# A Griffin block with two MLPs: the first chunk taken by pairs of token tiles, the second chunk's mixing put behind the first gate product

## The reference

```
t   = rmsnorm(x) * n1
xb  = causal_conv4(t @ Wx) + conv_b
r,i = sigmoid(xb @ Wa), sigmoid(xb @ Wi)
a   = exp(-8 * softplus(lam) * r)
h_t = a_t * h_(t-1) + sqrt(max(1 - a_t^2, 1e-12)) * i_t * xb_t
mix = (h * gelu(t @ Wy)) @ Wo ;  h1 = x + mix
u   = rmsnorm(h1) * n2
f   = (gelu(u @ Wg) * (u @ Wu)) @ Wd
x1  = layernorm(x + h1 + f)
out = layernorm(x1 + relu(x1 @ W1 + b1) @ W2 + b2)
```

## Time and profile before

| | us |
|---|---|
| median of 3 runs | 626.53 (626.53 to 627.58) |
| the profiled execution | 628.97 |
| its span | 627.2 |
| TensorE busy | 604.5 (96%) |
| VectorE busy | 386.0 (62%) |
| ScalarE busy | 305.7 (49%) |
| GpSimd busy | 204.4 (33%) |

### The profile page before, as it was taken

One profiled execution on the slowest core, in us unless ns is written; L12 is line 12 of the kernel. 1 busy time (PEld: TensorE's weight loads), 2 busy tenths in 40 slices (PEclk: granted clock), 3 DMA queues, 4 the chain that ended last, 5 costly groups with the idle time before them and its releaser, 6 DMA issues.

```text
span 627.2 us, 9436 instructions
## 1 busy us (share of the span) xinstructions
PE 604.5 (96%) x3633; PEld 537.1 (86%) x3633; DVE 386.0 (62%) x689; ACT 305.7 (49%) x564; POOL 204.4 (33%) x305
## 2 busy tenths in 40 slices
PE   7999988999999999999999999999999999999984
PEld 6898877788988898889888898889988898988974
DVE  5795665736485747747477566848368474562554
ACT  4774733366443754447443754438444653322341
POOL 4614117220724045140723125231531314240131
PEclk9999989999999999999999999999999999999998
DMA  8600001000000001010010101001000100010001
GB/s 276 219 2 33 1 2 34 0 1 2 33 1 1 33 1 36 2 34 0 1 34 2 34 1 34 0 1 35 2 1 0 34 2 1 0 35 1 1 33 35
DMA packets 13069, 15.69 MB, mean 25 GB/s; under 512 B 584, under 2 KB 12256, under 8 KB 13024
## 3 DMA queue, kind: packets, MB, share of 16 engines
q1 hardware_dynamic: 13024, 15.09, 7.1%
HBM read 10.89 MB, written 4.19 MB: 24 GB/s over the span
## 4 chain that ended last, share of the span: by engine, by line
PE 85%; DVE 8%; ACT 2%; POOL 2%; issue 2%; DMA 1%; POOLq 0%; ACTq 0%; DVEq 0%
PE psum L284 18%; PE psum L286 17%; PE psum L285 17%; PE psum L292 10%; PE psum L294 10%; PE psum L293 10%; PE psum L299 3%; DVE xb L733 1%; DVE row L808 1%; POOL normed L1047 1%; DVE xv L769 1%; DMA xs<-in_L_attn_x_dram 1%; DVE gu_raw L831 1%; POOL rstd L1016 1%; DVE sp L971 0%
## 5 line engine op out<-in xcount | busy, mean ns | idle before, releaser
L1076 POOL TENSOR_SCALAR gu_hi<-gu_raw 128x512 fp32r<-128x512 f32 x64 | 50.6, 791 | 320.0 <-DVE gu_raw L831 320.0
L841 DVE TENSOR_TENSOR hid_lo<-hid_raw,hid_hi 128x512 fp32r<-128x512 f32 x64 | 51.6, 807 | 97.1 <-ACT hid_hi L612 97.1
L608 ACT ACTIVATE hid_raw<-psum,vecs 128x512 f32<-128x512 f32 x64 | 43.9, 686 | 128.4 <-PE psum L286 128.3
L831 DVE TENSOR_TENSOR gu_raw<-psum,gu_raw 128x512 f32<-128x512 f32 x64 | 44.1, 689 | 81.5 <-PE psum L286 79.1
L292 PE MATMUL psum<-w_d_hi,gu_hi 128*128 128x256 f32 x256 | 73.2, 286 | 2.4 <-DVE gu_lo L836 2.4
L292 PE MATMUL psum<-w_hi,hid_hi 128*128 128x256 f32 x256 | 72.1, 282 | 2.4 <-DVE hid_lo L841 2.4
L294 PE MATMUL psum<-w_d_hi,gu_lo 128*128 128x256 f32 x256 | 72.4, 283 | 0.0
L293 PE MATMUL psum<-w_d_lo,gu_hi 128*128 128x256 f32 x256 | 72.1, 282 | 0.0
L294 PE MATMUL psum<-w_hi,hid_lo 128*128 128x256 f32 x256 | 71.9, 281 | 0.0
L293 PE MATMUL psum<-w_lo,hid_hi 128*128 128x256 f32 x256 | 71.8, 280 | 0.0
L599 ACT ACTIVATE gu_raw<-psum 128x512 f32<-128x512 f32 x64 | 38.0, 595 | 49.7 <-PE psum L286 49.0
(11 more groups left out here) (145 smaller groups left out, 1544.8 us busy)
## 6 DMA issues: line engine op xcount, KB each, us to landing
xs<-in_L_attn_x_dram SPq DMA_DIRECT2D x8, 512.0 KB, 3.5
out_dram<-row SPq DMA_DIRECT2D x16, 256.0 KB, 2.2
raw<-in_L_ffn_W_dram SPq DMA_DIRECT2D x2, 1024.0 KB, 13.0
raw_gud<-in_L_attn_Wg_dram SPq DMA_DIRECT2D x1, 1024.0 KB, 9.0
raw_gud<-in_L_attn_Wu_dram SPq DMA_DIRECT2D x1, 1024.0 KB, 11.0
raw_gud<-in_L_attn_Wd_dram SPq DMA_DIRECT2D x1, 1024.0 KB, 13.6
raw_xyai<-in_L_attn_Wx_dram SPq DMA_DIRECT2D x1, 256.0 KB, 2.7
raw_xyai<-in_L_attn_Wy_dram SPq DMA_DIRECT2D x1, 256.0 KB, 2.9
```

Of the source, the lines that this page charges most:

```text
L608: nc.scalar.activation(hid_raw[:, w % SLOTS, :], bank[:, :], ACT.Relu, bias=vec("b1", m)).then_inc(relu_ready, 1)
L831: nc.vector.tensor_tensor(gu_raw[:, r % SLOTS, :], up_bank(r)[:, :], gu_raw[:, r % SLOTS, :], ALU.mult).then_inc(gu_ready, 1)
L841: nc.vector.tensor_tensor(hid_lo[:, w % SLOTS, :], hid_raw[:, w % SLOTS, :], hid_hi[:, w % SLOTS, :].bitcast(FP32), ALU.subtract).then_inc ...
L1076: nc.gpsimd.tensor_scalar(gu_hi[:, r % SLOTS, :], gu_raw[:, r % SLOTS, :], 1.0, 0.0, ALU.mult, ALU.add).then_inc(gu_hi_ready, 1)
```

## The change

- x of the first chunk is loaded as two halves, each of two token tiles. Squares, mean and power, normalising (now on VectorE), transposes and splits go by such pairs, so that a bank holds both blocks of features of a pair (`transposed_by_pairs`, `split_hi_by_pairs`, `split_lo_by_pairs`, `pair_bank`). The same is done for u of the first chunk, normalised on ScalarE (`first_norm_u`).
- The order of the first chunk's products becomes x, decay, input, y. `first_decay` takes both outputs' first block ahead of the second; `first_out` does so for each pair of tiles. The convolution finishes feature block 0 before block 1's last taps.
- ScalarE does tanh, exp, tanh, square root and GELU of the first chunk in that order, and the square of the decay moves to VectorE (`squared_decay`).
- The splits of Wy, Wa, Wi, Wg and Wu move from GpSimd to ScalarE for their high part; the softplus steps and low parts are spread between VectorE's other steps.
- `mix_x(1)` goes between the gate and the up product of unit 0, `mix_y(1)` behind the up product, `mix_decay(1)` and `mix_input(1)` behind the products of round 2, `mix_out(1)` in round 6. `down(7)` goes ahead of `gate_up(8)`.
- Fillers, in steps of `keep_running`: 8, 14, 5, 9, 28, 24 before; 10, 8, 6, 9, 36, 28, 16, 6, 10 after.

The core of the diff:

```diff
+            def transposed_by_pairs(src, ready, done, bank, fillers):
+                for q in range(PAIRS):
+                    pe.wait_ge(ready, 2 * q + 2)
+                    for tt in (2 * q, 2 * q + 1):
+                        for f in range(KD):
+                            last = nc.tensor.transpose(pair_bank(bank, q)[:, f, (tt % 2) * P:(tt % 2 + 1) * P],
+                                                       src[:, tt, f * P:(f + 1) * P], ident[:, :])
+                    last.then_inc(done, 1)
+                    keep_running(fillers[q], DOWN)
...
+            def first_decay(bank):
+
+                for k in range(KD):
+                    pe.wait_ge(xb_lo_ready, k + 1)
+                    for m in range(KD):
+                        last = product_step(psum[bank + m][:, :], "a", m, k, mT_hi, mT_lo)
+                        if k == KD - 1:
+                            last.then_inc(wa_done, 1)
...
+                if r == 0:
+                    split_done("g")
                 product(gate_bank(r)[:, :], "g", m, uT_hi, uT_lo).then_inc(gate_done, 1)
+                if r == 0:
+
+                    mix_x(1)
+                    split_done("u")
...
+                if r == KH:
+
+                    down(r - 1)
                 if units(r):
                     gate_up(r)
+                if r == 0:
+                    pe.wait_ge(gy_ready, KD)
+                    mix_y(1, bank=DOWN)
+                if r == 2:
+                    mix_decay(1)
+                    mix_input(1)
+                if r == 6:
+                    mix_out(1)
...
-            transpose_t(0)
-            keep_running(5, SECOND)
+            transposed_by_pairs(normed, t_ready, tT_done, MIX, (6, 9))
             split_done("x")
             mix_x(0)
+            keep_running(36, SECOND)
+            split_done("a")
+            pe.wait_ge(vecs_ready, 1)
+            first_decay(GATE)
+            split_done("i")
+            mix_input(0, bank=SECOND)
+            transpose_t(1)
             split_done("y")
             mix_y(0, bank=DOWN)
-            transpose_t(1)
-            keep_running(9, SECOND)
-            split_done("a", "i")
-            pe.wait_ge(vecs_ready, 1)
-            mix_decay(0, bank=GATE)
-            mix_input(0, bank=SECOND)
-            mix_x(1)
-            pe.wait_ge(gy_ready, KD)
-            mix_y(1, bank=DOWN)
             pe.wait_ge(tanh_a_ready, KD)
             keep_running(28, GATE)
             split_done("o")
-            mix_out(0, bank=GATE)
             pe.wait_ge(tanh_i_ready, KD)
-            keep_running(24, SECOND)
-            transpose_u(0)
-            mix_decay(1, bank=SECOND)
-            pe.wait_ge(gy_ready, 2 * KD)
-            mix_input(1, bank=DOWN)
-            split_done("g", "u")
+            first_out(SECOND)
+            pe.wait_ge(gy_ready, KD)
+            keep_running(16, DOWN)
+            transposed_by_pairs(normed, u_ready, uT_done, GATE, (6, 10))
```

In the rounds, ScalarE and VectorE have:

```diff
                     if m == 0:
+                        conv_start(n, 0)
+                        conv_start(n, 1)
+                        gelu_y(n, bank=DOWN)
+                    if m == 1:
+                        weight_hi("2")
+                        xb_hi(n)
+                    if m == 2:
+                        tanh_decay(n)
                         exp_decay(n)
+                        tanh_input(n)
                         square_decay(n)
                         act.preload_act_table(ACT.Gelu_apprx_tanh)
...
                 if r == 0:
+                    convolve(n, 0)
+                if r == 1:
+                    convolve(n, 1)
+                if r == 3:
                     gated_input(n)
                 if r == 4:
+                    for k in range(KD):
+                        scan(n, k)
+                gate_lo(r)
+                if r == 1:
+                    convolve(n, 2)
+                    xb_lo(n)
+                if r == 2:
+                    weight_lo("2")
+                if r == 4:
                     gated(n)
+                if r == 5:
                     hy_lo(n)
                 if r == 7:
                     weight_lo("1", ks=[0])
```

More of the change, by code:

```diff
@@ L157, in griffin_mlp_kernel @@
         x_loaded = [sem(f"x_loaded{i}") for i in range(2)]
+        x0_loaded = [sem(f"x0_loaded{q}") for q in range(PAIRS)]
         out_stored = [sem(f"out_stored{i}") for i in range(2)]
@@ L325, in mix_x, with first_out @@
                     product(psum[MIX + m][:, :], "x", m, tT_hi, tT_lo).then_inc(wx_done, 1)
+            def first_decay(bank):
[5 more added lines that the diff above has]
+                            last.then_inc(wa_done, 1)
+            def first_out(bank):
+                for q in range(PAIRS):
+                    for k in range(KD):
+                        if q == 0:
+                            pe.wait_ge(hy_lo_ready, k + 1)
+                        for tt in (2 * q, 2 * q + 1):
+                            last = product_by_tokens(half_bank(bank, tt), "o", k, mT_hi[:, k, toks(tt)],
+                                                     mT_lo[:, k, toks(tt)], k == 0 and tt % 2 == 0, k == KD - 1)
+                    last.then_inc(wo_done, 1)
             def mix_decay(c, bank=MIX):
@@ L523, in split_hi, with split_hi_by_pairs @@
                     nc.scalar.activation(dst[:, f, :], psum[MIX + f][:, :], ACT.Copy).then_inc(ready, 1)
+            def split_hi_by_pairs(dst, bank, done, ready):
+                for q in range(PAIRS):
+                    act.wait_ge(done, q + 1)
+                    nc.scalar.activation(dst[:, :, half(q)], pair_bank(bank, q), ACT.Copy).then_inc(ready, 1)
             def conv_start(c, m):
@@ L723, in split_lo, with split_lo_by_pairs, first_norm_t, squared_decay @@
                                             ALU.subtract).then_inc(ready, 1)
+            def split_lo_by_pairs(dst, hi, bank, hi_ready, ready):
+                for q in range(PAIRS):
+                    dve.wait_ge(hi_ready, q + 1)
+                    nc.vector.tensor_tensor(dst[:, :, half(q)], pair_bank(bank, q), hi[:, :, half(q)].bitcast(FP32),
+                                            ALU.subtract).then_inc(ready, 1)
+            def first_norm_t():
+                for q in range(PAIRS):
+                    dve.wait_ge(rms1_rstd, q + 1)
+                    for tt in (2 * q, 2 * q + 1):
+                        nc.vector.tensor_scalar(normed[:, tt, :], xs[0][:, tt, :], rstd1[:, tt:tt + 1], None,
+                                                ALU.mult).then_inc(t_ready, 1)
+            def squared_decay():
+                dve.wait_ge(xtail_saved, 1)
+                for m in range(KD):
+                    dve.wait_ge(a_ready, m + 1)
+                    nc.vector.tensor_tensor(xv[:, m, 0:T], decay[:, m, :], decay[:, m, :],
+                                            ALU.mult).then_inc(a_squared, 1)
+                    room(0, [m])
             def convolve_half(c, step, m):
@@ L745, in xb_lo, with room @@
                                             ALU.subtract).then_inc(xb_lo_ready, 1)
-            def room(c):
-                for m in range(KD):
+            def room(c, ms=range(KD)):
+                for m in ms:
                     dve.wait_ge(a_squared, 2 * c + m + 1)
@@ L969, in _ @@
             lam_stepped(nc.vector.tensor_scalar(poly, z, 1.0 / 17.0, None, ALU.mult))
-            for odd in range(15, 1, -2):
+            for odd in range(15, 5, -2):
+                lam_stepped(nc.vector.scalar_tensor_tensor(poly, poly, 1.0 / odd, z, ALU.add, ALU.mult))
+            for step in range(LOOKBACK):
+                convolve_half(0, step, 0)
+            convolve_half(0, 0, 1)
+            weight_lo("a")
+            xb_lo(0, [0])
+            convolve_half(0, 1, 1)
+            convolve_half(0, 2, 1)
+            weight_lo("i")
+            xb_lo(0, [1])
+            for odd in range(5, 1, -2):
                 lam_stepped(nc.vector.scalar_tensor_tensor(poly, poly, 1.0 / odd, z, ALU.add, ALU.mult))
@@ L1129, in _ @@
             tail(0)
[L1131 to L1133 removed]
+            head(1)
+            first_rms(ss2, h1_squared, rms2_ms, rstd2, rms2_rstd)
             weight_hi("d")
[L1135 removed]
             tail(1)
[L1137 to L1138 removed]
             pool.wait_ge(b2_loaded, DMA)
```

232 lines of the change are left out of this document (126 added, 106 removed).

## The result

The changed kernel is slower: median 632.98 us (632.37 to 633.68, four runs) against 626.53 (626.0 to 627.58). The ratio is 1.0091, 95% interval 1.0067 to 1.0115. I had predicted 631.2, in a range of 625.6 to 634.6, and slower with a chance of 0.72.

What follows compares the result with a forecast made beforehand. TensorE, busy 96% of 627.2 us, bounds the kernel, fillers included. First gate product 50.9, work 51.4 and waits 8.5 put the third chunk's `mix_x` at 110.8 against 106.08: +4.7, so 631.2 us, range 625.6 to 634.6.

Steps and rivals of the forecast that it cites:

- The front: TensorE's timeline up to the first gate product, forecast at 50.9 against a level 47.1: a loss of 3.8 us.
- the wait for u: Ahead of the first chunk's u transposes, before the first gate product: TensorE waits 1.2 us for the first pair.
- the waits of the first rounds: First eight rounds, first gate product to `mix_x(2)`: seven waits sum to 7.65, with restarts 8.5, against 7.6 before.
- the first wait: `mix_decay(1)` in round 2 waits 1.6 us for VectorE's and GpSimd's chain, 5.76 against TensorE's 4.14.
- the last three: Waits at the end of the first eight rounds: down(7) 1.95, gate(8) 0.9, `mix_x(2)` 1.75 us.
- Three waits: In the first eight rounds: `mix_out(1)` 0.6, transposes of u(1) 0.35 (0 to 0.85), down(7) 1.95 us.
- the mark: Start of the third chunk's `mix_x`, 106.08 before, forecast 110.8; behind it the cost stays the same, 521.1 us.
- The gain of 1.7: `mix_x(0)` and `mix_y(0)` lasted 7.16 instead of 5.46 at 1.2 GHz; `mix_x(0)` was forecast at full clock.
- My 4.7: Forecast delay of the third chunk's `mix_x`: 50.9 + 51.4 + 8.5 = 110.8, against 106.08.
- Rival 1: The clock falls in the first rounds; one fall 1.7 us, two 3.4: 632.9 to 634.6 us, chance 0.17.
- Rivals 2 and 3: Second chunk's products cover old waits: below 2.6, 624.7 us, chance 0.16; no difference, waits 3.5 to 4.5, 626.5 us, 0.12.
- The table loads: ScalarE before the first gate product: four later loads become two, sparing 2.6 us at 1.28 each, hidden by fillers.

Runs made afterwards that it cites:

- the 59: All executions of the unchanged kernel before, run beside the follow-up experiments; their median is 627.74 us.

## Why the prediction was right, and where its size was off

- **The front loses 3.8 us against before.** Right. Predicted and measured starts: `mix_x(0)` 12.1 and 12.20, decay 22.95 and 22.99, `mix_out(0)` 38.55 and 38.33, the wait for u 1.2 and 1.03, first gate product 50.9 and 50.47. The loss in the traces is 3.4. The run with 16 fewer steps shows that the queue of fillers sets it: with 3.6 us of queue gone the gate product came 1.86 sooner, and only then did the chain hold it. The run without fillers had its gate product at 47.10, 3.4 sooner, though the mean clock was 0.50 to 0.68 in each window of 5 us from 30 on. The recorded 9.5 us for 82 more fillers are 9.3 at 0.113 each.
- **The second chunk's products do not fill the waits of the first rounds.** Right: 1.6, 0.5, 0.6, 0.35, 1.95, 0.9, 1.75 predicted; 1.71, 0.67, 0.16, 0, 1.41, 0.84, 1.57 measured. By order alone the first wait went in one run and the last three fell from 3.82 to 2.07 in another, so their cause is shown as well as their size.
- **Two slips inside that term.** The first wait's listed terms sum to 5.51, not 5.76, and the wait to 1.4. And the brackets sum to 6.36, the forecast waits to 7.65, yet the stretch is only 0.5 shorter than forecast (59.4 against 59.9): around each wait 0.27 are lost, as the run with the taps in round 0 shows, where I had put 0.12 for the restart. With that the six waits cost 8.0, against the forecast 8.5; the two errors partly cancel.
- **Three waits were too long in the forecast.** They were over by 0.35 to 0.55. The transposes of u(1) did not wait, likely because GpSimd's power ahead of them took 1.02, and 1.87 in the trace of before. For down(7) it is that the transposes then started 0.3 behind the last normalised tile and not with it, and that a bracket begins 0.17 behind the start that the next product could have had. For `mix_out(1)` the step is open.
- **Nothing behind the mark changes.** Right, 521.1 and 521.1.
- **The mis-sized term is the clock of the kernel before.** "The profiled execution took 628.97 ... The runs' median, 626.53, is 2.4 below that execution" carried the trace's difference of 4.7 over to the medians unchanged. The 2.4 were those slow stretches: the trace of before has two, its shorter executions by their mean clock one or none, and the changed kernel none. The gain of 1.7 that I gave the change in `mix_x(0)` was gained only where the clock had fallen. At a like clock the trace's 3.8 are 6.3, and the medians' 6.4 follow. My 4.7 was 0.9 too much for the traced pair (0.4 in the front, 0.5 in the rounds) and 1.7 too little for the medians. How far off it is depends on which executions of before it is held against: with the 59, at 627.74, it is 0.5 too little. That the time fell near the number therefore owes something to luck; the steps ahead of the mark do not.
- **Rival 1**, a fall in the new rounds, did not come: the trace of after has none, and the mean clock of its other executions is 0.996 to 0.998; waits up to 1.71 left the clock alone. **Rivals 2 and 3** needed the waits to be under 2.6 or 4.5; they sum to 6.4.
- The table loads: the row's 1.28 stood. No run shows what sparing ScalarE two of them is worth; TensorE had fillers there.

## What to carry to other kernels

Where fillers stand on the bound engine, count the whole queue, fillers included and in instructions rather than steps, before following any dependence: work moved away from a place that fillers then cover is paid twice. Fill a wait with the next stage's real products first, and trim fillers until a wait just shows. And before adding a gain read off one trace to a median, see whether every execution has it: mean clock and span of each run tell. To time on an engine that looks free, add what its work does to the engine beside it.

## What the runs showed of the hardware that I had not expected

- The same wait sometimes lets the clock fall and sometimes not: behind 1.83 it fell in the first trace of the kernel before and not in the second (1.84), behind 2.17 not and behind 2.19 it did. Behind waits of up to 1.72 it fell in no trace; behind 3.10 it did.
- VectorE and GpSimd beside each other: the squaring took 1.60 instead of 0.69, the step behind it, with one input, 1.23 instead of 0.43. GpSimd's power of two columns took 0.70 for the first pair of u and 1.62 for the second, both with VectorE at work; what makes the difference is not settled.
- With no fillers behind the small transpose the kernel ran at a mean clock of 0.975 to 0.980 and was as fast as with 119 more steps of them (632.5 against 632.98).
